# An AdaLN block with linear attention and a mixture of experts: the next chunk transposed first in a step, and the routing chain further forward

## The reference

```
h = layernorm(x) * (1 + ca) + sa
x = x + ga * attention(h)          # 16 heads of 16, causal, linear
h = layernorm(x) * (1 + cb) + sb
x = x + gb * ffn(h)                # one shared expert and the best 2 of 8
```

## Time and profile before

| | |
|---|---|
| median of 3 runs | 954.58 us (954.52 to 955.95) |
| the profiled execution | 953.07 us |
| its span, first to last instruction | 951.3 us |
| PE busy | 860.2 us (90%) |
| DVE busy | 815.7 us (86%) |
| ACT busy | 489.8 us (51%) |
| POOL busy | 408.3 us (43%) |
| mean granted clock of PE | 0.964 |

### The profile page before, as it was taken

How to read it: one execution, slowest core, us unless ns; L and a number is a source line. 1 busy time by engine, 2 the same in 40 slices (tenths; PEclk the granted TensorE clock), 3 DMA queues, 4 the chain that set the end, 5 groups by cost and what they waited for, 6 DMA issues and landing times. The chain is left out here.

```text
span 951.3 us, 14272 instructions
## 1 busy us (share of the span) xinstructions
PE 860.2 (90%) x4377; PEld 648.6 (68%) x4377; DVE 815.7 (86%) x1263; ACT 489.8 (51%) x860; POOL 408.3 (43%) x502
## 2 busy tenths in 40 slices
PE   5766739999999999999999999999999999979998
PEld 4545427676767676786767676777767676756786
DVE  2696979999989998999989998999999998889423
ACT  4634546555556656655656566566556563441321
POOL 2341444363636355453636254543646253463220
PEclk9975769999999999999999999999999999999999
DMA  8014134453533535453534445354634243443422
GB/s 309 1 29 89 45 68 145 86 153 76 137 92 77 153 79 160 86 155 70 153 77 96 130 87 165 68 155 90 162 71 133 66 100 113 78 133 83 117 79 55
DMA packets 51705, 100.34 MB, mean 105 GB/s; under 512 B 5380, under 2 KB 34127, under 8 KB 49623
## 3 DMA queue, kind: packets, MB, share of 16 engines
q1 hardware_dynamic: 36356, 66.14, 21.2%
q0 software_dynamic: 14832, 33.03, 20.2%
q10 hardware_dynamic: 482, 0.74, 0.2%
HBM read 57.68 MB, written 17.06 MB: 79 GB/s over the span
## 5 line engine op out<-in xcount | busy, mean ns | idle before, releaser
L1487 PE MATMUL acc<-w,hid 128*128 128x256 f32 x1128 | 262.5, 380 | 2.6 <-DVE hid L1169 2.6
L1487 PEld LDWEIGHTS acc<-w,hid 128*128 128x128 f32 x1128 | 213.9, 190 | 37.6 <-DVE hid L1169 4.7
L845 ACT ACTIVATE hid<-ring,b1row 128x512 f32<-128x512 f32 x144 | 98.7, 685 | 143.0 <-PE ring L1368 140.4
L1169 DVE TENSOR_TENSOR hid<-hid,cfw 128x512 f32<-128x512 f32 x128 | 111.1, 870 | 37.0 <-DMA cfw<-cf_rows 21.6
L665 POOL DMA_DIRECT2D feat<-feat x48 | 43.7, 910 | 228.8 <-DVE feat L1046 115.0
L800 ACT ACTIVATE feat<-ring,bqkv 128x512 f32<-128x512 f32 x96 | 65.7, 686 | 81.9 <-PE ring L1368 81.9
L1368 PE MATMUL ring<-n2H,w1H 128*128 128x512 f32 x288 | 102.5, 437 | 0.0
L1445 PE MATMUL tr<-wo_g,feat 128*128 128x256 f32 x256 | 65.3, 413 | 35.9 <-DVE feat L1088 35.9
L1021 DVE TENSOR_TENSOR_SCAN feat<-zero,carry,feat 128x512 f32<-128x512 f32 x80 | 97.1, 1261 | 0.0
L1021 DVE TENSOR_TENSOR_SCAN feat<-zero,feat 128x512 f32<-128x512 f32 x80 | 95.7, 1243 | 0.0
L1368 PE MATMUL ring<-n2H,w1L 128*128 128x512 f32 x288 | 90.8, 397 | 0.0
(11 more groups left out here) (171 smaller groups left out, 1559.8 us busy)
## 6 DMA issues: line engine op xcount, KB each, us to landing
feat<-feat POOLq DMA_DIRECT2D x48, 512.0 KB, 4.6
cfw<-cf_rows SPq DMA_DIRECT2D x16, 1280.0 KB, 7.6
xin<-in_L_attn_x SPq DMA_DIRECT2D x16, 512.0 KB, 9.3
feat<-inv_rows SPq DMA_DIRECT2D x32, 256.0 KB
cfw<-cf_rows SPq DMA_DIRECT2D x16, 512.0 KB, 3.6
out<-x SPq DMA_DIRECT2D x15, 512.0 KB, 8.5
out<-fin POOLq DMA_DIRECT2D x15, 512.0 KB, 6.0
cfw<-cf_rows SPq DMA_DIRECT2D x16, 256.0 KB, 4.5
```

The source lines that it names most:

```text
L845: a.activation(hid[:, e % NG], ring[bank][:, :], ACT.Silu, bias=b1row[:, e:e + 1]).then_inc(ring_copied, 1)
L1169: v.tensor_tensor(hid[:, e % NG], hid[:, e % NG], cfw[:, (e - 1) % NW], ALU.mult).then_inc(hidw_ready, 1)
L1487: last = mm(acc[t // 2][:, t % 2], hid[:, e % NG, t * P:(t + 1) * P], w2[:, e], start=False, stop=(e == E), skip_group_check=True)
```

## The change

On PE `transposes(0, nxt)` moves to the start of the step, ahead of the first up products, and waits for the two halves of `residual` one by one. `transposes(1, prev)` moves from behind `expert(1)` to behind `expert(0)`, ahead of the projections. `route_logits` stands between the projections q0 and q1, `logits_by_token` behind q1, and `expert(1)` and `expert(2)` follow together. `combine_by_expert` moves from the end of the step to a place ahead of `expert(8)`.

On ACT `highs(0)` opens the step, `normalise_second` for all four token groups stands between `silu(0)` and `silu(1)` where it was interleaved with the copies of k and q, and `highs(1)` and `copy_logits` move forward with the products. `combine_rows` stands ahead of `normalise_first`.

On DVE `lows(0)` follows the statistics directly, `lows(1)` moves ahead of `weigh(2)`, and the three routing functions move forward by one to three experts. On POOL `exps`, `scores` and `split_weights` move ahead of the second and third addition of orders and of `inv_std_of_squares`. `inv_std` stays as it was: ten operations on POOL. A tile `mean_var` and four semaphores are declared that nothing uses.

```diff
@@ buffers and semaphores @@
+        mean_var = sb("mean_var", [P, NT, 2])
+        aggregate_begun, aggregated, mean_var_ready, second_pow = (
+            sem(f"second_{n}") for n in ("aggregate_begun", "aggregated", "mean_var", "pow"))
@@ POOL, step @@
                 if st["norm"]:
                     token_means(pool, *later(i, p, 2))
+                if st["second"]:
+                    exps(*later(i, p, -1))
+                    scores(*later(i, p, -1))
                 if st["attn"]:
                     add_orders(i, p, 1)
+                if st["second"]:
+                    split_weights(*later(i, p, -1))
                 if st["norm"]:
                     inv_std_of_squares(pool, *later(i, p, 2))
-                if st["second"]:
-                    exps(*later(i, p, -1))
                 if st["attn"]:
                     add_orders(i, p, 2)
-                if st["second"]:
-                    scores(*later(i, p, -1))
-                    split_weights(*later(i, p, -1))
@@ ACT, step @@
-                silu(0)
-                silu(1)
                 if qkv:
                     highs(0, *nxt)
+                silu(0)
+                if second:
+                    for t in range(NT):
+                        normalise_second(act, *prev, t)
+                silu(1)
                 silu(2)
                 if attn_:
                     scale_even(i, p)
-                for t, half in enumerate(HALVES[:4]):
-                    copy(half)
-                    if second:
-                        normalise_second(act, *prev, t)
-                silu(3)
                 if second:
                     highs(1, *prev)
-                silu(4)
+                for half in HALVES[:3]:
+                    copy(half)
                 if second:
                     copy_logits(*prev)
+                copy("q1")
+                silu(3)
+                silu(4)
...
                 silu(8)
+                if second:
+                    combine_rows(*prev)
                 if st["norm"]:
                     normalise_first(act, *later(i, p, 2))
...
-                if second:
-                    combine_rows(*prev)
@@ DVE, step @@
                     token_stats(dve, 1, *prev)
+                if qkv:
+                    lows(0, *nxt)
                 if attn_:
                     odd(i, p, 1)
                     weigh(i, p, 0)
-                if qkv:
-                    lows(0, *nxt)
-                if attn_:
                     weigh(i, p, 1)
                     prefix(i, p, 0)
...
                 expert(1)
+                if second:
+                    lows(1, *prev)
                 if attn_:
                     weigh(i, p, 2)
                 expert(2)
                 if attn_:
                     prefix(i, p, 1)
-                if attn_:
                     carry_over(i, p, 0)
-                if second:
-                    lows(1, *prev)
-                if attn_:
                     order_product(i, p, 0)
                     order_product(i, p, 1)
                 expert(3)
+                if second:
+                    logit_parts(*prev)
                 if attn_:
                     weigh(i, p, 3)
                     prefix(i, p, 2)
                     prefix(i, p, 3)
                 expert(4)
+                if second:
+                    softplus(*prev)
                 if attn_:
                     carry_over(i, p, 1)
                     order_product(i, p, 2)
                     order_product(i, p, 3)
                 if second:
-                    logit_parts(*prev)
+                    combine_weights(*prev)
...
                 expert(5)
-                if second:
-                    softplus(*prev)
...
                 expert(8)
-                if second:
-                    combine_weights(*prev)
@@ PE, transposes @@
                 if behind_norm:
                     pe.wait_ge(low_ready[0], 2 * (c + 3))
-                else:
-                    ge(pe, x1_ready, 2 * (c - 1 if n == 0 else c + 1))
+                elif n:
+                    pe.wait_ge(x1_ready, 2 * (c + 1))
                 for k in range(KD):
+                    if n == 0:
+                        ge(pe, x1_ready, 2 * (c - 1) - 1 + k)
                     for t in range(NT):
@@ PE, step @@
+                if isinstance(i, int) and number(i, p) == 0:
+                    late_products_of_mods()
+                if qkv:
+                    transposes(0, *nxt)
                 if ffn:
                     expert_up(*exp, use, 0)
                     expert_up(*exp, use, 1)
                     second_biases(*exp)
-                if isinstance(i, int) and number(i, p) == 0:
-                    late_products_of_mods()
-                if qkv:
-                    transposes(0, *nxt)
                 expert(0)
-                if qkv:
-                    for half in HALVES[:4]:
-                        project(*nxt, use, half)
-                expert(1)
                 if second:
                     transposes(1, *prev, behind_norm=qkv)
-                expert(2)
+                if qkv:
+                    for half in HALVES[:3]:
+                        project(*nxt, use, half)
                 if second:
                     route_logits(*prev)
+                if qkv:
+                    project(*nxt, use, "q1")
+                if second:
+                    logits_by_token(*prev)
+                expert(1)
+                expert(2)
                 if attn_:
                     head_sums(i, p, 0, second)
-                if second:
-                    logits_by_token(*prev)
-                if attn_:
                     head_sums(i, p, 1, second)
...
                 expert(7)
+                if second:
+                    combine_by_expert(*prev, attn_)
                 expert(8)
...
                 if attn_:
                     project_out(i, p)
-                if second:
-                    combine_by_expert(*prev, attn_)
```

## The result

The changed kernel takes 1075.89 us (median of 4 runs, 1072.25 to 1076.80), the kernel before beside it 954.55 us: a ratio of 1.126, interval 1.123 to 1.130. The forecast was 977 us and its range ended at 1003. The direction was right; the loss is 121 us and not 22.

The account below looks back on a forecast made before the run. PE, 90% busy, was taken to bound the kernel, now waiting early for the second norm. Full steps +14.8, last steps +5 and step 1 +2 gave 22 us on 953.07: 975, plus 1.5 for the median, 977 us; range 957 to 1003.

Parts of the forecast that it names:

- The chain's length: GpSimd's ten `inv_std` operations for the second norm: 5.45 us, bounds 4.1 and 6.6, the last three meeting DVE's block.
- +14.8: Loss in us forecast for the 13 full steps, at 54.1 us a step; with the bounds -2.7 and +29.8.
- Rival 1: Longer than forecast: chain starved in DVE's block, +35 to +48 us, or PE's clock falls; 985 to 1010 us; chance 0.19.
- I: Length of GpSimd's second-norm chain in a step; a step equals the old 52.93 us at 4.3 us.
- The routing chain and the third addition: Moved routing hidden in full steps; third DMA addition landing about when needed, within a risk of up to 1 us a step.
- T: Start of the first operation (L353) of GpSimd's second-norm chain, from which the forecast measures times in a step.
- `project_out` waits for nothing: Sign of a right forecast: PE idles before `transposes(1)` and q0 instead, together 1.5 to 4 us.
- PE's formula, 48.62 + I: Length of a full step in us, from PE's work and ScalarE's path between the chain and q0.
- rival 3: Faster: DVE stops behind `lows(0)`, chain 2.86 us, a step 51.5, full steps -18.9; 940 us; chance 0.08.
- The clock hidden: PE's slower clock after a stall, 1.7 us each, would mostly hide behind ScalarE, as q0 waits for a copy.
- The ends: Partial steps outside the 13 full ones: about +5 us in steps 15 to 17, about 2 in step 1.
- First chunk's transposes ahead of the up products: Start of PE's step: the split wait in `transposes(0)` saves nothing, its wait of about 0.4 us covered by k0's later start.

Follow-up runs that it names:

- lows_late: The changed kernel with `lows(0)` back behind `weigh(0)` on DVE; 1051.84 us, ratio 1.102.
- hold_split_late: hold with `combine_by_expert` and `combine_rows` back in their old places and `split_weights` behind the third addition; 1014.05 us, ratio 1.061.
- add_first: The changed kernel with the third addition ahead of `inv_std_of_squares` on POOL; 1063.10 us, ratio 1.115.
- hold: The changed kernel with DVE waiting behind `lows(0)` until GpSimd's ten-operation chain of the second norm is through; 1044.43 us, ratio 1.092.
- route_old: The changed kernel with all of the routing back in its old places, early transposes and logits kept; 1012.51 us, ratio 1.050.
- w5: hold_route_old with GpSimd's `weigh_order_5` also waiting until `lows(1)` is written; 977.18 us, ratio 1.021.
- filler: The changed kernel with 20 products that nobody reads on PE ahead of `transposes(1)`; 1072.13 us, ratio 1.122.
- first_hold: first_only plus DVE's wait behind `lows(0)` until GpSimd's chain is through; 971.53 us, ratio 1.015.
- hold_route_old: The changed kernel with the routing in its old places and DVE held behind `lows(0)` until the chain is through; 983.00 us, ratio 1.027.
- first_only: The kernel before with `transposes(0)` and `highs(0)` opening the step and `lows(0)` behind the statistics, nothing else; 963.02 us, ratio 1.007.

## Why the prediction was wrong, step by step

1. **The chain's length (mis-sized).** The forecast took 5.45 us with bounds 4.1 and 6.6; it is 8.28 and 9.41, mean 8.85, beyond both. The start was right: six (or five) operations run in 0.20 us each beside `lows(0)`. What failed: the forecast had seven through and let the power meet the block, with about one DVE operation of waiting for each of the last three; in fact the sixth or seventh is caught, and it waits out the whole row of four or five. The trace of before showed it. Its chain at 462.51 has a first operation of 3.29 us, and DVE beside it:

```profile
462.26 1.21 DVE L984 SCALAR_TENSOR_TENSOR feat<-feat 128x1024 f32<-128x1024 f32 x1
463.38 1.22 DVE L986 SCALAR_TENSOR_TENSOR feat<-feat 128x1024 f32<-128x1024 f32 x1
464.52 1.22 DVE L1002 TENSOR_TENSOR feat<-feat 128x1024 f32<-128x1024 f32 x1
465.65 1.40 DVE L968 SCALAR_TENSOR_TENSOR n1L<-tr,mods,n1H 128x512 fp32r<-128x512 f32 x2
```

That operation ended at 465.80, when the row of three was through and `lows(0)` had begun. 3.29 us is no property of the operation but the length of that row; the change takes `lows(0)` out of the middle and makes the row four or five long (put back, lows_late: 24 us). Why some operations get in between two of DVE's, as at 410.59, stays open. How far the chain is when a row begins is not all of it: with `odd` begun 0.17 us ahead, L353 took 1.10 us at 515.87 and 3.37 at 778.43, both in the kernel before.

By the formula the step becomes 48.62 + 8.85 = 57.5 us, 13 steps +59 in place of +14.8. Rival 1 named this mechanism, at I of 7 to 8, and counted on no more than that.
The Trainium skill (GPSIMD Engine Reference, Key points), that GpSimd contends with instructions that have two SBUF inputs, agrees in kind. Reading it as one whole operation of waiting for each of three did not: one waited for four to five, the ones behind it for one or none.

2. **The routing chain and the third addition (the step that failed most).** Counted at nothing, with up to 1 us a step as its risk; with the chain held it costs 62 us, nearly 5 us a step. The text did see that the addition would be issued about 41 us after T and land just as it is needed. It went out 42.5 to 45.6 us after T (505.70 - 462.86 = 42.8 in the step shown), and two things were missed. First, DVE's own routing functions, `logit_parts` and `softplus`, moved ahead of the order product, push the second addition too: it goes out 5.2 to 6.1 us ahead of the inverse's end, before 7.8 to 8.0, and in hold_split_late the third is seen waiting for its landing. The prediction weighed DVE's moves for `cfw`, where they arrive, and not for the additions, which they displace. Second, its price for a late addition was a wait of `finish_numerator`; that the addition in flight makes the inverse's own way longer (add_first) was not in it. `inv_std_of_squares`, which also stands ahead of the addition and which the text doesn't name, took 1.9 to 2.6 us, much as before (2.2 from 440.66 to 442.84); in three of hold's full steps it met DVE and took 4.9.

3. **"`project_out` waits for nothing": wrong.** It waits 41.3 us. Point 2 is why: `divide` starts 9.7 us after the inverse on average, not 7.2, and with the routing back (route_old) `project_out` waits at most 1.0 us in each full step, in most of them not at all.

4. **PE's formula, 48.62 + I: right** where the routing is back in its place (route_old, within 1.7 us a step but for step 2). Its floor was missed: with a short chain `route_logits` waits for `lows(1)`, and with that wait mostly gone (w5) DVE's `divide` is late. I = 2.87 gives 54.60 and 54.1 us a step, not 51.5, so rival 3's 940 us did not come. (Both have the hold, which costs DVE time of its own.)

5. **The clock hidden: right as far as filler shows,** a few us at most; whether behind ScalarE, as the text has it, or behind the late additions, it doesn't tell. `transposes(1)` does take 1.93 us in place of 1.04 behind an idle time of 4.51.

6. **The ends.** +5 for the last steps and +2 for step 1 were forecast; +12.0 and +9.6 came. The waits of DVE in step 15, some 7 us forecast, are 5.07 + 2.35 = 7.42:

```profile
957.48 0.69 DVE L1174 TENSOR_TENSOR hid<-hid,cfw 128x512 f32<-128x512 f32 x1 [5.07 <-ACT hid L848]
...
960.52 1.41 DVE L973 SCALAR_TENSOR_TENSOR n2L<-tr,mods,n2H 128x512 fp32r<-128x512 f32 x2 [2.35 <-ACT n2H L791]
```

But they arise otherwise: PE waits 6.84 us there for a chain of 9.17 us. From the start of step 14's `project_out` to the end it was 124.5 us before and is 134.8 now; first_hold has 126.0, hold_route_old 130.5, route_old 134.6. So some 4 us each belong to the chain and to the second transposes, and none to the routing. From step 0's `project_out` to step 1's it was 53.0 us before and is 58.1 after, 54.0 in route_old, 56.1 in hold and 52.2 with both: there the routing has some 4 us and the chain 2, and the sum of step 1 had only the chain. Of the other 4.5 us of the start, 3.5 lie ahead of step 0's `project_out` (85.72 before, 89.22 after); filler, the same kernel up to there, has 85.22, so they are no price of the change.

7. **First chunk's transposes ahead of the up products: counted at nothing, +6 us** (first_only).

## What to carry to other kernels

When a chain of small operations on one engine is made critical, look at what the neighbour issues back to back beside it, and price the caught operation at the whole run of work without a gap, not at one instruction of it. When work is moved forward on a queue, list what it is moved past and follow each of these to its consumer: here the routing, moved past two DMA additions, cost more (62 us by the sum) than the chain that the change was about (33). A formula for one engine's path has a floor where the next engine's path takes over; before a rival is priced with it, ask which product then waits for what.

## What the runs showed of the hardware

- A GpSimd operation on 128x4 values takes 0.20 us alone, and in the changed kernel 4.66 or 5.78 us when it starts within 0.05 us of the start of a row of DVE operations on 128x1024 tiles: it ends 0.2 us into the first scan, or as the second begins. Where the row starts 0.2 to 0.4 us later (first_only), the chain is through in 3.85 to 4.94 us. It is not so without exception: in step 5 of route_old the seventh operation started 0.02 us behind `odd` and took 1.29 us.
- It goes both ways: `odd` beside GpSimd's 128x1024 `weigh_order_5` (505.11, 2.39 us) took 3.27 us in place of 1.22, and ended 1.08 us after that had.
- In the full steps of all 17 traces, where the third DMA addition is sent 1.0 us ahead of the inverse's end or later, it takes 8.05 to 12.2 us from there to `divide`; 6.9 to 8.5 where it is sent 2.6 us ahead or earlier. (One step lies between: 1.7 us ahead, 8.5.) In the 22 steps in which it is sent 0.6 to 1.0 us ahead, the inverse's write is held: SyncE's read behind it goes out 4.0 to 5.4 us after the inverse's end, 0.2 to 0.3 us after the addition has landed, and 2.0 us after that end in the 16 steps in which the addition was sent 3.7 us ahead or earlier. Where the addition is sent after the write (0.5 us and more behind the inverse's end, 82 steps), the read goes out at 2.0 to 2.2 us, and the landing of the read or of the addition is what comes late. Whether they meet in a queue or in the DMA engines is not shown.
